# A five-engine program whose step order is drawn anew

## The reference

```python
# L0_attn: a selective scan (Mamba); 512 channels, 16 states
hidden, gate = split(x @ in_proj_w)
u = silu(causal_conv(hidden)) ; dt, B, C = split(u @ x_proj_w)     # rms-normed
dt = softplus(dt @ dt_proj_w)
s_t = exp(dt * A) * s_(t-1) + (dt * u) * B_t      # for each channel and state
y_t = sum over states of s_t * C_t ;  out = ((y + u*D) * silu(gate)) @ out_proj_w
# L0_ffn: causal attention whose result only modulates a gated MLP
mod = 0.1 * tanh(attention(norm(x)) @ A)
x = x + (silu(h @ W_in + mod * (h @ A) @ B) * (h @ W_up)) @ W_down
# L1_attn: gated linear attention (GLA), 4 heads, chunks of 64, output norm and gate
# L1_ffn: mixture of experts: softmax router, top 4, silu(x@gate) * (x@up) @ down
```

## Time and profile before

| | us |
|---|---|
| median of three runs | 2918.93 (2915.26 to 2927.77) |
| the profiled execution | 2919.7 |
| its span | 2918.0 |
| PE busy in it | 2434.3 (83%) |
| DVE busy | 2118.6 (73%) |
| ACT busy | 1419.2 (49%) |
| POOL busy | 636.6 (22%) |

### The profile page before, as it was taken

One profiled execution on the slowest core, in us unless ns is written; L12 is line 12 of the kernel. 1 busy time (PEld: TensorE's weight loads), 2 busy tenths in 40 slices (PEclk: granted clock), 3 DMA queues, 4 the chain that ended last, 5 costly groups with the idle time before them and its releaser, 6 DMA issues.

```text
span 2918.0 us, 37858 instructions
## 1 busy us (share of the span) xinstructions
PE 2434.3 (83%) x12823; PEld 1509.9 (52%) x12823; DVE 2118.6 (73%) x3010; ACT 1419.2 (49%) x2325; POOL 636.6 (22%) x611
## 2 busy tenths in 40 slices
PE   5787798889879888889888888888779897998991
PEld 3764355545544455445544554455435544556880
DVE  3889975898669967896789677976797652246666
ACT  5866345735571556255735563546435326333340
POOL 2002001300240015010320233111500313025661
PEclk8998799969985999699978997899879999978995
DMA  2112220223031312141222211321233174365757
GB/s 105 66 56 99 87 78 9 94 89 112 17 97 60 109 62 83 39 143 63 65 83 95 88 58 53 131 87 30 73 107 100 36 160 162 103 197 153 225 178 306
DMA packets 138314, 288.72 MB, mean 99 GB/s; under 512 B 14208, under 2 KB 83344, under 8 KB 137872
## 3 DMA queue, kind: packets, MB, share of 16 engines
q1 hardware_dynamic: 124304, 247.76, 26.3%
q0 software_dynamic: 13824, 38.55, 3.6%
HBM read 216.72 MB, written 69.54 MB: 98 GB/s over the span
## 4 chain that ended last, share of the span: by engine, by line
PE 50%; DVE 21%; ACT 11%; issue 8%; POOL 6%; DMA 2%; SPq 1%; DVEq 0%; POOLq 0%; ACTq 0%; PEldq 0%
PE bank L2257 10%; DVE scan L1690 5%; PE bank L2516 5%; PE bank L2270 4%; PE bank L2455 4%; PE bank L2471 3%; PE bank L2435 3%; PE bank L2806 3%; DVE rest L1846 3%; ACT rest L1433 2%; PE bank L2244 2%; PE bank L2542 2%; DVE scan L1699 2%; PE bank L2827 2%; DVE scan L1686 2%
## 5 line engine op out<-in xcount | busy, mean ns | idle before, releaser
L1690 DVE TENSOR_TENSOR_SCAN scan<-scan 128x1024 f32<-128x1024 f32 x224 | 516.3, 2305 | 46.2 <-ACT scan L1389 40.7
L1389 ACT ACTIVATE scan<-scan 128x511 f32<-128x511 f32 x512 | 339.4, 714 | 384.1 <-DVE scan L1690 366.4
L2435 PE MATMUL bank<-ident,scan 128*128 128x128 f32 x2048 | 306.3, 303 | 85.4 <-DVE scan L1699 77.2
L2435 PEld LDWEIGHTS bank<-ident,scan 128*128 128x128 f32 x2048 | 261.0, 157 | 149.8 <-DVE scan L1699 79.1
L1699 DVE TENSOR_TENSOR scan<-scan 128x1024 f32<-128x1024 f32 x256 | 320.4, 1252 | 5.0 <-DVE rest L1881 1.0
L2516 PE MATMUL bank<-rest 32*128 32x384 f32 (+3 forms) x1024 | 268.1, 636 | 50.8 <-DVE rest L1846 37.4
L1714 DVE TENSOR_TENSOR scan<-scan 128x1024 f32<-128x1024 f32 x224 | 277.7, 1240 | 9.7 <-PE bank L2435 5.0
L1029 POOL DMA_INDIRECT rows_dram<-stage,slot_at x128 | 177.7, 1388 | 461.9 <-DVE chosen L1793 345.3
L1007 POOL TENSOR_SCALAR rs<-mv 128x4 f32<-128x4 f32 x24 | 21.1, 878 | 1087.6 <-DVE off L1601 1086.9
L1846 DVE TENSOR_REDUCE rest<-bank 128x2 f32<-128x1024 f32 (+3 forms) x176 | 195.7, 1123 | 49.6 <-PE bank L2521 47.9
L1433 ACT ACTIVATE rest<-bank 128x2048 f32<-128x2048 f32 (+3 forms) x128 | 158.3, 1237 | 140.6 <-PE bank L2542 140.4
(11 more groups left out here) (399 smaller groups left out, 4439.8 us busy)
## 6 DMA issues: line engine op xcount, KB each, us to landing
scan<-bc_dram SPq DMA_DIRECT2D x240, 512.0 KB, 3.8
wslot<-wt SPq DMA_DIRECT2D x64, 384.0 KB, 3.1
rows_dram<-scan SPq DMA_DIRECT2D x32, 670.0 KB, 4.1
scan<-y_dram SPq DMA_DIRECT2D x32, 512.0 KB, 10.0
rest<-rows_dram SPq DMA_DIRECT2D x108, 134.0 KB, 2.8
scan<-rows_dram SPq DMA_DIRECT2D x52, 134.0 KB, 3.2
scan<-wt SPq DMA_DIRECT2D x4, 1536.0 KB, 15.9
wslot<-x SPq DMA_DIRECT2D x8, 512.0 KB, 3.7
```

The source lines that it names most:

```text
L1389: i = a.activation(decay[:, unit % 2, n, 1:], dt[:, c, 1:], ACT.Exp, scale=a_neg[:, c, 2 * pair + n:2 * pair + n + 1])
L1690: d.tensor_tensor_scan(flat, decay[:, unit % 2].rearrange("p n t -> p (n t)"), flat, 0.0, ALU.mult, ALU.add).then_inc(decay_used.sem, 1)
L2435: m = t_.matmul(A.bank(("yT", c))[:, t * P:(t + 1) * P], drive[:, unit % NDRIVE, n, t * P:(t + 1) * P], ident[:, :], is_transpose=True, st ...
```

## The change

The lists in `ORDER` are replaced, for all five engines. No step, operation, tile, buffer or semaphore is added, removed or altered, each list has as many steps of each column as before, and within a column the steps keep their order. So only how the three columns interleave on each engine differs. POOL's list, whole:

```diff
     "POOL": (
-        "X4 R3 X1 R1 U10 R4 U6 X1 U11 R1 U5 X3 R2 X2 R5 X1 R1 X2 U4 R1 X1 U4 X1 R5 X2 R1 U8 X1 U3 R1 X1 U5 X1 "
-        "R4 U7 R1 X3 R1 U9 R1 X2 R4 U2 R1 X1 U1 X1 U3 R1 U3 X1 U2 R1 X1 U9 X1 R5 X3 R1 U12 R1 X1 U1 X1 R6 X3 "
-        "U10 R1 U13 R5 U1 R1 X23 U1 X7 R1 X13 R1 X5 R2 X3 R1 X4 R1 U1 X1 R1 X4 R1 X2 "
+        "R3 X1 R3 U10 X2 U5 R2 X2 U6 X1 R1 X1 R1 X2 R1 X2 R4 U7 R1 U3 R1 X3 U2 R1 U3 X1 U8 X1 R4 U1 R1 U1 X2 "
+        "U1 R1 X1 U14 R1 X2 R5 U2 R1 X3 U10 R1 X1 U2 X1 R4 U2 R1 U2 R1 X3 U14 R1 X2 R5 U2 X1 R1 X2 U15 R1 X2 "
+        "R5 U1 X3 R1 U2 R1 U2 X1 U3 X1 U1 R4 U8 R2 X2 U2 X24 R1 X10 R2 X1 U1 R1 X4 R1 X12 R2 X4 R1 X3 U1 "
     ),
```

Of the lists of PE and DVE, the lines in which turn 3's MLP ends (DVE: R523 is the add to xb, X95 the statistics of a_stats, U468 to U477 the last units of the scan; PE: R809 is the last matmul of the MLP, U206 to U212 the last sums), and DVE's first line, with X11, the first statistics of the front of turn 1; "..." stands for the other lines:

```diff
     "PE": (
...
-        "U1 R1 U1 R4 U1 R3 U1 R1 U1 R3 U1 R9 U2 R7 U1 R16 U4 R2 X2 R4 X1 R1 X1 R2 U1 X2 R1 U2 R7 X1 R1 X1 R8 "
+        "U1 R6 U2 R6 U1 R2 U1 R2 U1 R8 U1 R1 U1 R1 U1 R2 U1 R2 U1 R3 U1 R3 U1 R4 U2 R2 U1 R8 U2 R2 U1 X1 R1 X1 "
...
     "DVE": (
-        "R6 X1 R12 U1 X6 R13 U26 R31 U1 R10 U2 R4 U1 X3 U1 X2 U4 R13 U3 R8 U5 X2 U4 X1 U1 R8 U3 X1 R1 U3 R1 U6 "
+        "R3 X2 U1 X1 U1 R18 X2 R1 X7 R1 U2 R1 U1 R2 U7 R1 U8 R2 U14 R3 U7 X1 U3 X2 U8 R1 U3 R37 X1 U2 R27 U10 "
...
-        "R1 U2 R3 U5 R2 U4 R5 U5 R1 U2 R4 U1 R2 U1 R3 U1 R10 U1 X1 U8 R1 X2 U1 R2 X2 R8 X1 R4 X1 R8 U2 X2 U1 "
+        "R1 U1 R2 U1 R2 U1 R2 U2 R7 X1 U1 R1 X2 R1 X1 R2 X1 R9 X1 R4 X1 U1 R6 X1 R1 X2 U1 X1 U1 R1 X2 R1 U1 R1 "
...
```

## The result

| | us |
|---|---|
| before, median (4 runs beside the kernel after) | 2917.1 |
| after, median (4 runs) | 2958.1 |
| ratio, 95% interval | 1.0148 [1.0111, 1.0185] |
| the profiled execution of after, its span | 2958.8, 2957.0 |

What follows compares the result with a forecast made beforehand. No engine was full: DVE was busiest in attention, PE filled the MLP, and behind it work passed between engines. From 2919.7 us, -20.3 - 0.3 - 2.0 + 1.8 gave 2898.9, as median 2898; range 2866 to 2930.

Steps and rivals of the forecast that it cites:

- the MLP pays and is not paid back: Slower rival: sums moved into the full MLP wait for late DVE products, little returns behind it; 2945 us, chance 0.16.
- PE's sums: In the MLPs: 36 sums of 0.87 us move in, where PE has no idle time; 31.3 us added.
- The DVE steps among them must fit the MLP: Turn 3's MLP: DVE's moved scans and products fit, 40.7 of 44.2 us, by little; costed at nothing.
- Against that, behind the MLP, the scan is over sooner: Behind the MLP: chain steps and POOL's power freed, 5.9 us a turn in turns 1 to 5; 31.6 us back.
- The scatters: Start of attention: fewer scatters ahead of t_rs on POOL shorten DVE's wait; three quarters of 27 us, 20.3 gained.
- What is late next in turns 4 and 6 is ACT's own queue: Start of attention: with scatters moved, ACT's queue is the next delay, so not all of the 27 us need arrive.
- The prologue: Before the first scan: X11's statistics move into DVE's idle 10.38 us; 2.0 us gained, or 0.
- ACT's table loads: On ACT: 13 more loads, 200 instead of 187, 16.7 us of ACT; 11% taken, 1.8 us added.

Runs made afterwards that it cites:

- scatters_early: Kernel before with only POOL's list changed: in turns 2 to 7 all scatters behind attention's statistics go ahead of them; 2879.9 us, ratio 0.9898.
- the joined parts: Kernel before with the new prologue, the new order from turn 7's MLP to the end, and all scatters ahead of attention's statistics; 2868.0 us, ratio 0.9873.
- after_pool: Kernel after with POOL's remaining scatters ahead of attention's statistics and gate products of turns 1, 3, 4, 5 ahead of the memsets; 2898.6 us, ratio 0.9959.

## Why the prediction was wrong

The forecast missed by 60 us of the profiled execution. The rival that came nearest was the first, "the MLP pays and is not paid back" (2945), by its place; not by its mechanism, a DVE that comes late in the MLP: that rival had 21 us for it, and PE idles 3.9 us more in the seven MLPs.

- **PE's sums, +31.3: right.** PE has 34.0 us more to do in the seven MLPs and idles 3.9 more: +37.9.
- **"The DVE steps among them must fit the MLP": right.** 42.24 of 51.20 us in turn 3.
- **"Against that, behind the MLP, the scan is over sooner", 31.6 back: the step that failed most.** It came to +4.2 (-12.2, and +16.4 in turns 0 and 6). Its items show in the trace: U468 is gone from between the statistics, and a_rs takes 0.19 and 1.01 us instead of the 1.00 and 2.88 of the earlier trace rows:

```profile
1384.88 0.19 POOL L1011 TENSOR_SCALAR a_rs<-a_mv 128x4 f32<-128x4 f32 x1 [0.44 <-DVE a_off L1605]
1385.16 1.01 POOL L1013 TENSOR_TENSOR a_rs<-a_rs,minus_half 128x4 f32<-128x4 f32 x1
```

  The front's norm reaches PE 10.4 us behind the add to xb in turn 3 instead of 13.4, so 3.0 of these 3.8 us do arrive there. What the sum lacked is that the sums in front of GLA also helped to keep TensorE at its upper clock. In turn 6 their removal leaves PE idle 3.46 us, and GLA runs at 0.50 for 27 us instead of at 1.00 for 17, ten us; with the gap filled by five matmuls it runs at the upper clock again. That the forecast met these ten us in full is partly bad luck: the old order loses the clock there in some traces too (the table above), and the profiled execution of before is not one of them. In turns 1 to 5 the gain is large just where the old order had a dip of the clock at GLA already: from the add to xb to the next statistics 4.7, 3.1 and 4.8 us in turns 3, 4 and 5, but 1.3 and -0.6 in turns 1 and 2, where it had none; in turn 2 the 8 us ahead of GLA have 0.74 (1097.50 above) where they had 1.00. Turn 0, whose stretch is 4.7 us longer, has a clock of 0.85 instead of 0.91 in it. All this but turn 6 is read from the traces and was not tried alone.
- **The scatters, -20.3: right about the wait, wrong about the new list.** Alone they give -30. The prediction counted the scatters that leave POOL's queue ahead of t_rs (29 us of issue) and not those that stay or come: two behind t_rs in each of turns 2 to 6, and U61 and U62, which go the other way. ACT waits until the last has landed, in the kernel before as well (turns 2, 5 and 6), so the end of the queue decides, and not how many are gone from it. In turns 2 to 6 the new attentions gained 3.9 us; with the rest of the scatters gone too they gain 57 more.
- **"What is late next in turns 4 and 6 is ACT's own queue": wrong in the new order.** In the kernel after it was POOL's queue and the landing still. In scatters_early, where POOL was early, `stage` stands behind ACT's own work in turn 4 and DVE waits 1.9 us; in turn 6 ACT waits 2.15 us for POOL, and DVE not at all.
- **The prologue, -2.0: not told apart from the measured** -7 [-12, -1]. X11 stands at 60.30 us, ahead of the first scan, as forecast.
- **ACT's table loads, 1.8: as counted,** 13 instructions more (2338 instead of the 2325 in the earlier trace rows); what they cost was not tried.
- **Not priced at all:** the attentions of turns 0 and 1, +13.6. In turn 1 DVE idles 17.7 us instead of 10.3, and all six traces with the new attentions take 158.9 to 160.7 us there, the ten others 150.9 to 151.4; the new list puts the row maxima ahead of the scan's products, but which step does it was not tried. Nor were the weights of turn 7 priced, +8.5 by the trace.

## What to carry to other kernels

What a moved instruction did for its old neighbours belongs in its price: on PE, work in a gap keeps the clock up for what follows, and two unread matmuls in one turn's gaps brought 11 us behind them, while seven in every turn, more than turn 6's gap held, cost 42 in all. Where an engine waits for the last of a queue, count what is left in the queue and not what was taken out. And try the parts of a large change alone: here two of four lost and two gained, and the largest gain came from one engine's list alone. Before a stretch is compared in two traces, look at the same steps in a third: the clock alone moved turn 6's stretch by 12 us.

## What the runs showed of the hardware

- TensorE's clock can fall with hardly a gap. In the joined parts it fell at 2259 us, behind waits of 0.67, 0.83, 0.23 and 1.30 us, and stayed at 0.50 for 24 us in which PE did not idle. In the kernel before the same waits stand ahead of the same matmuls to within 0.1 us, and it did not fall. The rule quoted above, of idle gaps, does not tell the two apart. What does was not found; it is worth 12 us in one turn.
- A small power on POOL takes 1.01 us where DVE idles and 2.88 beside its scan; a product of 128x512 there 1.28 and up to 3.25. Where POOL was early, moving these products changed the time by nothing that shows (after_pool).
- An unread float32 matmul of 128x512 shows as two passes of 0.44 us, 0.88 in all (fourteen passes took 6.17).
